# Second attention: attended values and their copy ahead of the second query product

## The reference

```python
xn, ln = layernorm(ctx), layernorm(layernorm_plain(x))      # media and latents
q = (ln @ Wq + bq) * DH ** -0.5                             # 8 heads of 128
k, v = split(concat([xn, ln], 1) @ Wkv + bkv)               # 64 + 64 = 128 keys per batch
attn = softmax(einsum('bhid,bhjd->bhij', q, k))
out = einsum('bhij,bhjd->bhid', attn, v)
x = x + tanh(g_xattn[1]) * (out.reshape(b, 64, 1024) @ Wo + bo)
```

## Time and profile before

| | us |
|---|---|
| median of 3 runs (lowest, highest) | 1474.5 (1474.22, 1475.13) |
| the profiled execution | 1471.77 |
| its span, first to last instruction | 1470.1 |
| second attention, about | 1000 to 1312 |
| busy in the span: PE, ACT, DVE, POOL | 1372.0, 1014.4, 953.2, 528.5 |
| mean granted TensorE clock, share of full speed | 0.987 |

### The profile page before, as it was taken

One profiled execution on the slowest core, in us unless ns is written; L12 is line 12 of the kernel. 1 busy time (PEld: TensorE's weight loads), 2 busy tenths in 40 slices (PEclk: granted clock), 3 DMA queues, 4 the chain that ended last, 5 costly groups with the idle time before them and its releaser, 6 DMA issues. The chain is left out here.

```text
span 1470.1 us, 33716 instructions
## 1 busy us (share of the span) xinstructions
PE 1372.0 (93%) x12029; PEld 1168.6 (79%) x12029; DVE 953.2 (65%) x2359; ACT 1014.4 (69%) x2019; POOL 528.5 (36%) x525
## 2 busy tenths in 40 slices
PE   5888699999999999999999999997999999979995
PEld 5787588888888888888888888886788888757874
DVE  6998766766766766667667666644355555557555
ACT  4887588676677676776776776655788888745552
POOL 3111454333322322423233222212234555555764
PEclk9999899999999999999999999999999999999998
DMA  8300100009998000000000000004000000012336
GB/s 220 94 1 1 59 2 1 2 2 169 188 41 99 2 2 1 2 2 2 2 2 2 2 2 2 1 1 131 1 30 9 16 16 16 21 44 79 92 104 185
DMA packets 124980, 60.46 MB, mean 41 GB/s; under 512 B 41945, under 2 KB 120241, under 8 KB 124690
## 3 DMA queue, kind: packets, MB, share of 16 engines
q1 hardware_dynamic: 120274, 48.92, 18.3%
q0 software_dynamic: 4544, 9.38, 1.9%
HBM read 28.84 MB, written 29.44 MB: 40 GB/s over the span
## 5 line engine op out<-in xcount | busy, mean ns | idle before, releaser
L1354 DVE SCALAR_TENSOR_TENSOR hidden<-psU,b_cols,gelu 128x512 f32<-128x512 f32 x256 | 191.4, 750 | 169.8 <-ACT gelu L1479 95.4
L1479 ACT ACTIVATE gelu<-psG,b_cols 128x512 f32<-128x512 f32 x256 | 176.5, 689 | 104.2 <-PE psG L142 91.6
L1299 POOL TENSOR_TENSOR combine_sum<-combine_sum,combineT 128x512 f32<-128x512 f32 x48 | 63.6, 1325 | 288.4 <-ACT combineT L1493 288.4
L1326 POOL TENSOR_TENSOR dispatchT<-dispatchT,dispatch_inv 128x512 f32<-128x512 f32 x64 | 67.8, 1059 | 232.5 <-DVE dispatch_inv L1456 232.5
L1613 PE MATMUL psU<-w_down,hidden 128*64 128x128 f32 x2048 | 123.4, 273 | 0.0
L1613 PE MATMUL psDown<-w_down,hidden 128*64 128x128 f32 x2048 | 122.7, 273 | 0.0
L1866 POOL TENSOR_TENSOR probs<-probs,row_sum 128x512 f32<-128x512 f32 x64 | 66.4, 1037 | 143.5 <-DVE row_sum L1979 143.3
L1613 PEld LDWEIGHTS psU<-w_down,hidden 128*64 128x64 f32 x2048 | 113.2, 137 | 1.3 <-issue 1.2
L1613 PEld LDWEIGHTS psDown<-w_down,hidden 128*64 128x64 f32 x2048 | 113.9, 137 | 0.1
L2043 ACT ACTIVATE probs<-psS,neg_max 128x128 f32<-128x128 f32 x256 | 91.4, 385 | 22.7 <-DVE neg_max L1976 22.4
L140 PE MATMUL psG<-slots_hi,w_gate_hi 128*128 128x512 f32 x256 | 106.0, 414 | 1.3 <-ACT gelu L1479 0.8
(11 more groups left out here) (406 smaller groups left out, 3614.7 us busy)
## 6 DMA issues: line engine op xcount, KB each, us to landing
sorted_x<-empty_rows SPq DMA_DIRECT2D x1, 12736.0 KB, 73.2
tile_rows<-sorted_x SPq DMA_DIRECT2D x78, 65.0 KB, 1.9
sorted_x<-empty_rows SPq DMA_DIRECT2D x1, 4544.0 KB, 28.4
expert_ys<-expert_y SPq DMA_DIRECT2D x16, 256.0 KB, 5.5
x<-in_x SPq DMA_DIRECT2D x8, 256.0 KB, 5.4
ctx<-in_ctx SPq DMA_DIRECT2D x8, 256.0 KB, 5.4
w_gate_raw<-in_L_ffn_Wg SPq DMA_DIRECT2D x1, 2048.0 KB, 10.6
w_up_raw<-in_L_ffn_Wu SPq DMA_DIRECT2D x1, 2048.0 KB, 15.8
```

The lines of the kernel that those rows point to most:

```text
L1326: pool.tensor_tensor(e[:], e[:], over(rb[:], SEQ, 2), ALU.mult).then_inc(s["eb_normed"], 1)
L1354: dve.scalar_tensor_tensor(hid[e][:, half, :], U[half][:], bcol[:, 1, 4 * ch + 2 * e + half:][:, 0:1], gel[half][:], ALU.add, ALU.mult).th ...
L1479: act.activation(gel[half][:], G[half][:], ACT.Gelu, bias=bcol[:, 0, 4 * ch + 2 * e + half:][:, 0:1]).then_inc(s["gelu"], 1)
```

## The change

In slots 2 and 4 of octets that have values to make and prepare the next octet (`early_values`), the values product goes ahead of the slot's second query product on TensorE, and the copy yT goes ahead of the second query copy on ScalarE. In slots 3 and 5 (where an out product stands between) and everywhere else the order stays. The bodies of both steps and of the out product are put in functions of their own; `heavy` is the old condition with a name.

```diff
--- before.py
+++ after.py
@@ -1813,6 +1813,14 @@
         def parity(par, j, back):
             return par if j >= back else 1 - par
 
+        def heavy(o, j):
+
+            return 2 <= j <= 5 and has_head(o)
+
+        def early_values(o, j):
+
+            return heavy(o, j) and j % 2 == 0 and has_core(o) and exists(o, j, 3)
+
         def slots(eng, slot):
 
             def body(o, par):
@@ -2031,9 +2039,17 @@
                 act.activation(qT[1 - par][:, :, h, :], Q[:].rearrange("p (b n) -> p b n", b=OB), ACT.Identity,
                                bias=cq[:, h:h + 1], scale=SCALE).then_inc(s["q_ready"], 1)
 
+            def values_kept(o, j):
+
+                m = (j - 3) % OB
+                need(act, s["av"], o * OB + j - 2)
+                need(act, s["out"], 4 * o + (j - 3) // 2 - 1)
+                act.copy(yT[(m // 2) % 2][:, :, (m % 2) * SEQ:(m % 2 + 1) * SEQ],
+                         Y[:].rearrange("p (h n) -> p h n", h=H)).then_inc(s["yT"], 1)
+
             def slot(o, par, j):
                 n = o * OB + j
-                if 2 <= j <= 5 and has_head(o):
+                if heavy(o, j):
                     q_out(o, par, 2 * (j - 2))
                 if exists(o, j, 0):
                     need(act, s["neg_max"], n + 1)
@@ -2046,15 +2062,12 @@
                     need(act, s["tp"], n - 1)
                     need(act, s["av"], n - 3)
                     act.copy(pT[j % 2][:], T[:].rearrange("p a b -> p (a b)")).then_inc(s["probsT"], 1)
-                if 2 <= j <= 5 and has_head(o):
+                if early_values(o, j):
+                    values_kept(o, j)
+                if heavy(o, j):
                     q_out(o, par, 2 * (j - 2) + 1)
-                if exists(o, j, 3):
-
-                    m = (j - 3) % OB
-                    need(act, s["av"], n - 2)
-                    need(act, s["out"], 4 * o + (j - 3) // 2 - 1)
-                    act.copy(yT[(m // 2) % 2][:, :, (m % 2) * SEQ:(m % 2 + 1) * SEQ],
-                             Y[:].rearrange("p (h n) -> p h n", h=H)).then_inc(s["yT"], 1)
+                if exists(o, j, 3) and not early_values(o, j):
+                    values_kept(o, j)
                 if j == 0 and has_head(o) and has_core(o):
                     media_in(o, par)
                     latents(o)
@@ -2140,8 +2153,26 @@
                 product3(pe, Q[:], [w[:, h, :] for w in a], [w[:].rearrange("p b n -> p (b n)") for w in lat]
                          ).then_inc(s["q"], 1)
 
+            def out_product(o, j):
+                m = ((j - 5) % OB) // 2
+                t = 4 * o + (j - 5) // 2
+                need(pe, s["yT"], o * OB + j - 3)
+                need(pe, s["x_new"], t)
+                for h in range(H):
+                    last = pe.matmul(O[:, 0:D], yT[m % 2][:, h, :], bh[:, h, :], start=(h == 0), stop=(h == H - 1))
+                last.then_inc(s["out"], 1)
+
+            def values(o, par, j):
+                n = o * OB + j
+                need(pe, s["probsT"], n - 2)
+                need(pe, s["kvN"], o + (1 if j >= 3 else 0))
+                need(pe, s["yT"], n - 3)
+                pe.matmul(Y[:], kvN[parity(par, j, 3)][:, (j - 3) % OB, :], pT[(j - 3) % 2][:], start=True, stop=True
+                          ).then_inc(s["av"], 1)
+
             def slot(o, par, j):
                 n = o * OB + j
+                to_out = j % 2 == 1 and exists(o, j, 5)
                 if exists(o, j, 0):
                     if (o, j) == (0, 0):
                         pe.wait_ge(s["bh_ready"], 2)
@@ -2154,33 +2185,25 @@
                                          qT[par][:, j, 2 * hp:2 * hp + 2, :].rearrange("p h n -> p (h n)"),
                                          kvT[par][:, j, :], start=True, stop=True)
                     last.then_inc(s["scores"], 1)
-                if 2 <= j <= 5 and has_head(o):
+                if heavy(o, j):
                     if j == 2:
                         need(pe, R.s["copied"], o - 1)
                         need(pe, R.s["wd_ready"], min(o - 3, 4))
                     q_in(o, par, 2 * (j - 2))
-                if j % 2 == 1 and exists(o, j, 5):
-                    m = ((j - 5) % OB) // 2
-                    t = 4 * o + (j - 5) // 2
-                    need(pe, s["yT"], n - 3)
-                    need(pe, s["x_new"], t)
-                    for h in range(H):
-                        last = pe.matmul(O[:, 0:D], yT[m % 2][:, h, :], bh[:, h, :], start=(h == 0), stop=(h == H - 1))
-                    last.then_inc(s["out"], 1)
+                if to_out:
+                    out_product(o, j)
                 if exists(o, j, 2):
                     need(pe, s["normed"], n - 1)
                     need(pe, s["probsT"], n - 2)
                     for hp in range(HP):
                         last = pe.transpose(T[:, hp, :], pr[(j - 2) % 4][:, hp, :], c.ident[:])
                     last.then_inc(s["tp"], 1)
-                if 2 <= j <= 5 and has_head(o):
+                if early_values(o, j):
+                    values(o, par, j)
+                if heavy(o, j):
                     q_in(o, par, 2 * (j - 2) + 1)
-                if exists(o, j, 3):
-                    need(pe, s["probsT"], n - 2)
-                    need(pe, s["kvN"], o + (1 if j >= 3 else 0))
-                    need(pe, s["yT"], n - 3)
-                    pe.matmul(Y[:], kvN[parity(par, j, 3)][:, (j - 3) % OB, :], pT[(j - 3) % 2][:], start=True, stop=True
-                              ).then_inc(s["av"], 1)
+                if exists(o, j, 3) and not early_values(o, j):
+                    values(o, par, j)
                 if due("logits", o, j) is not None:
                     need(pe, R.s["wd_ready"], min(o - 3, 4))
                     R.tensor_logits(pe, due("logits", o, j), Q)
```

## The result

The changed kernel takes 1480.49 us (median of 6 runs, 1479.18 to 1483.06) against 1474.61 us (6 runs, 1473.13 to 1475.13) for the kernel before: 5.9 us or 0.36% slower, a ratio of 1.0036 with an interval of 1.0025 to 1.0047. The forecast was 1478.5 us, slower, with a range of 1475.6 to 1481.0.

The account below looks back on a forecast made before the run. TensorE sets the stage's pace overall, but ScalarE's chain sets the distance between query products. 8 x 0.47 = 3.76 us plus 5 x 0.04 = 0.20 us gave +4.0 us on 1474.5, so 1478.5 us, range 1475.6 to 1481.0.

Parts of the forecast that it names:

- The chain on ScalarE: From an even slot's first query product to the next odd slot's: copy, four exponentials, probsT, copy; 4.27 us, becoming 4.74.
- The stricter of the two: Claim from octet 0, slot 2: ScalarE, not TensorE, sets the query product distance; 4.28 us despite 0.86 us less TensorE work.
- Short places: Slot 4 of octet 0, two of octet 1, slot 2 of octets 2 to 6: 4.27 us distances, each +0.47 us.
- long places: Slot 4 of octets 2 to 6, with rank products between: distances of 4.69 to 4.70 us becoming 4.74, each +0.04 us.
- The five places with slack: Slot 4 of octets 2 to 6: rank products on TensorE cover almost all of the 0.47 us, leaving 5 x 0.04 us.
- everything after 1315 us is only moved: Sign for the profile after: the part behind 1315 us starts later but is otherwise unchanged, adding nothing to the +4.0 us.
- copies that do not overlap: Dearer case at the moved yT copy on ScalarE: 0.62 instead of 0.47 us, 5.9 us in all, 1480.4 us.
- slack that is missing: Dearer case in slot 4 of octets 2 to 6: no cover, so 13 x 0.47 = 6.1 us, 1480.6 us.
- Faster: Rival at the third and seventh query products: the filled TensorE gap counts, 5.6 to 7.7 us gained; chance 0.07.
- No change by other waits: Rival: TensorE's waits for yT before out products in slots 7 and 1 swallow the delay; 1474.5 to 1476.5 us; chance 0.16.
- Slower by more: Rival: moved copies cost 0.62 us each or slot 4's slack gives no cover; 1480.4 or 1480.6 us; chance 0.09.
- the 7.7 us: Gain if filling TensorE's gap before the second query product were all: 13 x 0.59 us, giving 1466.8 us.

Follow-up runs that it names:

- copy-first version: Changed kernel's TensorE order, with ScalarE's second query copy ahead of the probsT and yT copies; 1473.16 us against 1477.39 for the kernel before, ratio 0.9977.

## Why the prediction was right, and where it was not

**The chain on ScalarE** held at every place. The prediction read it from octet 0, where TensorE had 0.86 us less to do and was no sooner, and from a third product that began exactly one handover after the copy. TensorE's move alone left the short distances at 4.27 us; ScalarE's move alone lengthened all of them to 4.95 us. "The stricter of the two" it was by 0.02 us only: with its copy made earlier, the distance stayed at TensorE's own 4.25 us.

**The sizes.** Short places 4.75 to 4.76 us against 4.74 forecast, long places 4.76 against 4.74; the yT copy 0.47 us against 0.47; the stage +4.0 to +4.3 us against +4.0. The five places with slack cost 0.05 each, and doing only these gave +0.1 to +0.2 us in the stage.

**Terms of the working that were off.** The values product and the query product behind it take 0.60 + 0.96 = 1.56 us together, where I had put 0.86 + 0.77 = 1.63 from rows in which they stand the other way round. TensorE therefore comes earlier to a wait that ends at the same time: by starts the wait is 1.16 us instead of 1.06 (scores at 1139.47, the product 0.83 us behind them as in the earlier trace rows, so 1140.30 against 1141.46), of which 0.94 are printed, and the total is 11.4 us instead of "some 10". It costs nothing here.

**The step that failed** is "everything after 1315 us is only moved". In two profiles of the changed kernel the last stretch is 2.3 to 3.0 us longer than in three of before. Of this, about 2.2 us is TensorE's work between the second and the third group of tiles, which falls on the lower clock because the full one is back only 12.7 to 13.0 us behind the first transposes, not 6.7 to 6.9; the rest is mostly in front of the second group, where its rows are waited for. Why the clock comes back later stays open. With this term the stretches add up to 6.3 to 7.3 us; the rounds measured 5.9 and 3.5 us. As shares their intervals are 0.25% to 0.47% (3.7 to 6.9 us) and 0.09% to 0.36% (1.3 to 5.3 us), and the second leaves 6.3 us out. So it is not shown that the term is there in every execution of the changed kernel. The forecast of 4.0 lies between the two rounds, and their difference is nearly as large as the term; the marks inside the profiles show it, the medians alone would not.

That the 1480.49 us lies inside the range is in part luck: the range went up to 1481.0 us for copies that do not overlap and for slack that is missing, and neither came true. What filled it, as far as the profiles tell, was a term that the working had put at nothing.

**The rivals.** *Faster* (5.6 to 7.7 us) falls: the gap was filled in all 13 places, and the stage became longer. *No change by other waits* falls: the wait for yT is 8.4 us, 13 times, in both. *Slower by more* has its time about right but not its reason, since neither the copies failed to overlap nor was the slack missing.

**The rule that spoke against the forecast.** The Trainium skill, "Perfetto Trace Analysis", section Optimization Strategy, says to find the gaps on the most-contended engine and to make what they wait for begin or end sooner. It does not say that other work in the gap is a gain; the 7.7 us were my own reading. The change filled the gap without making the first query copy, for which it waited, any sooner, and made the second one, for which the next product waits, later: +4.0 us. The copy-first version fills the gap and makes the second copy sooner, and there the trace agrees with the rule: printed waits of 1.5 us instead of 7.1, and a stage 5.4 us shorter. The same copy made sooner without the filled gap gained nothing.

## What to carry to other kernels

Where two engines hand one buffer back and forth, add up both chains from one handover to the next, and look for a place in the trace that has less work on one of them: if it is no faster there, the other chain sets the pace. A gap that is filled with work gains only what that other chain allows, and a copy that frees the shared buffer belongs ahead of copies that nobody waits for yet. When two chains are level, shortening either alone may show nothing while both together do: in the 8 short places here each alone gave 0.00 to 0.02 us and both gave 0.47 us. So test such pairs together before giving one up.

## What the runs showed of the hardware

- Whole executions differ by several us already ahead of the changed part (first mark 1024.9 to 1030.8 us in 13 profiles), while the stage of one kernel repeats to 0.2 us. A part of 4 us is better read from marks within a profile than from medians.
- With nearly the same idle times at the beginning of the last stage (2.4 us, then 2.45 to 2.69 us), the granted clock stayed at its lower level for 6.8, 10.2 or 13.6 us and was back in full 6.7 to 13.2 us behind the first transposes. The same work behind them took 5.90 to 6.19 us when it was back early and 8.17 to 8.38 us when it was late. Adding 2.7 us of work ahead of it made the stretch behind 2.2 us shorter.
- A product of 128x512 in full fp32 hands over to a three-matmul product after 0.60 us, and that product's first matmul then takes 0.50 us; in the other order the first matmul takes 0.31 us and the fp32 product 0.86 us. The order changed their sum by 0.07 us.
